# Attention with a feed-forward layer: quad 0's stack of x for the next batch is loaded once x's parts are stored, no longer once q's parts are stored as well

## The reference

```
x = x + attn(layernorm(x));   x = x + ffn(layernorm(x))
attn:  x_h = 16 heads of width 16;  q = x_h @ w_att[h] / sqrt(16)
       att = softmax(q @ x_h^T);  o = att @ (x @ wv^T + b);  o @ out_w^T + out_b
ffn:   silu(fp4(x) @ fp4(w_gate)^T) * (fp4(x) @ fp4(w_up)^T)  ->  fp4(h) @ fp4(w_down)^T
```

## Time and profile before

| | us |
|---|---|
| median of 3 runs | 1467.87 (1466.48 to 1468.46) |
| profiled execution | 1475.75 |
| its span, first to last instruction | 1473.8 |

### The profile page before, as it was taken

How to read it: one execution, slowest core, us unless ns; L and a number is a source line. 1 busy time by engine, 2 the same in 40 slices (tenths; PEclk the granted TensorE clock), 3 DMA queues, 4 the chain that set the end, 5 groups by cost and what they waited for, 6 DMA issues and landing times. The chain is left out here.

```text
span 1473.8 us, 32381 instructions
## 1 busy us (share of the span) xinstructions
PE 1425.4 (97%) x8612; PEld 891.5 (60%) x8612; DVE 1264.4 (86%) x2652; ACT 865.5 (59%) x1731; POOL 659.0 (45%) x911
## 2 busy tenths in 40 slices
PE   6789999999999999999999999899999999999999
PEld 4445555555555555555555554577777777777776
DVE  6878888888888888888888887599999999999996
ACT  1667777777777767777777777533333333333332
POOL 2445545545545546546545523243434343433332
PEclk8999999999999999999999999999999999999999
DMA  7846456455455455465465353000000000000000
GB/s 204 234 132 190 123 144 180 122 154 180 122 154 168 132 155 161 123 166 162 125 165 145 117 145 84 0 15 15 18 14 18 14 18 14 18 14 18 14 18 22
DMA packets 99785, 148.09 MB, mean 100 GB/s; under 512 B 21024, under 2 KB 58272, under 8 KB 99744
## 3 DMA queue, kind: packets, MB, share of 16 engines
q1 hardware_dynamic: 82672, 137.22, 32.9%
q10 hardware_dynamic: 17072, 10.37, 3.0%
HBM read 85.02 MB, written 65.27 MB: 102 GB/s over the span
## 5 line engine op out<-in xcount | busy, mean ns | idle before, releaser
L1189 DVE TENSOR_REDUCE neg_max<-ring 128x1 f32<-128x512 f32 x1016 | 636.3, 680 | 96.2 <-PE ring L919 95.8
L1071 ACT ACTIVATE probs<-scores 128x512 f32<-128x512 f32 x1024 | 533.9, 604 | 184.3 <-PE scores L930 158.4
L1704 PE MATMUL gu_bank<-splits,f_x_T 128*128 128x352 f32 x1024 | 313.7, 459 | 0.1
L919 PE MATMUL ring<-x_stack,q_stack 64*128 64x512 f32 x1016 | 230.1, 449 | 24.5 <-DVE neg_max L1189 11.4
L952 PE MATMUL ring<-probs,v_quad 128*32 128x512 f32 x2048 | 247.9, 602 | 0.2
L1704 PEld LDWEIGHTS gu_bank<-splits,f_x_T 128*128 128x128 f32 x1024 | 189.6, 190 | 95.3 <-ACT f_x_T L1678 0.5
L927 PE MATMUL scores<-q_stack,x_stack 64*128 64x512 f32 x1024 | 207.9, 399 | 10.6 <-DMA max_stack<-max_rows 8.2
L919 PEld LDWEIGHTS ring<-x_stack,q_stack 64*128 64x128 f32 x1016 | 97.8, 186 | 177.2 <-DVE neg_max L1189 114.2
L930 PE MATMUL scores<-max_stack,max_ones 64*128 64x512 f32 x1024 | 203.9, 391 | 0.0
L1394 POOL TENSOR_TENSOR f_small<-f_small,eps 128x1 f32<-128x1 f32 x64 | 43.0, 671 | 296.0 <-DVE f_small L1361 296.0
L1663 ACT ACTIVATE h_T<-h_bank 128x256 f32<-128x256 f32 (+1 forms) x128 | 56.0, 487 | 169.9 <-PE h_bank L1718 169.9
(11 more groups left out here) (144 smaller groups left out, 2014.1 us busy)
## 6 DMA issues: line engine op xcount, KB each, us to landing
x_rows<-splits SPq DMA_DIRECT2D x128, 256.0 KB, 3.9
x_stack<-x_rows SPq DMA_DIRECT2D x126, 256.0 KB, 4.0
q_stack<-q_rows SPq DMA_DIRECT2D x248, 128.0 KB, 4.0
q_rows<-splits SPq DMA_DIRECT2D x64, 256.0 KB, 2.2
out_dram<-x_all SPq DMA_DIRECT2D x64, 128.0 KB, 1.7
x_all<-in_L_attn_x_dram ACTq DMA_DIRECT2D x14, 512.0 KB, 6.9
w_raw<-slabs SPq DMA_DIRECT2D x14, 192.0 KB, 4.0
slabs_kept<-w_turned SPq DMA_DIRECT2D x14, 192.0 KB, 6.1
```

What stands on the lines that cost most here:

```text
L919: pe.matmul(max_bank(b, g, ROWS * n + m)[:, :], row_tile(q_stack[q], m)[:, p, s * P:(s + 1) * P], row_tile(x_stack[q], m)[:, p, :], start= ...
L1071: act.activation(probs[j][:, k, :], scores[k][:, :], ACT.Exp).then_inc(p_ready, 1)
L1189: dve.tensor_reduce(neg_max[q % 2][:, at:at + 1], max_bank(b, g, k)[:, :], AX.X, ALU.max, negate=True).then_inc(m_used, 1)
L1704: m = pe.matmul(gu_bank[c][:, :], x_T[u][:, a, :], gate_up_T[:, a, c * CH:(c + 1) * CH], start=(a == 0), stop=(a == HALVES - 1))
```

## The change

For g = 0 only, SP's stream is written out anew. The four x stores come first, as before. Then SP waits until these four have landed (`stored[0]` at the batch's base plus `X_STORES` = 64), and only then waits for q's parts and stores them. After the wait for `s_ready` it loads x_stack[0] at once; then it waits until all six stores have landed, and loads q_stack[0]. For g = 1, 2 and 3 the stream is as it was. No transfer is added or taken away, and no other engine's stream is touched.

```diff
     LOAD_MAXIMA = 2
+    X_STORES = 4 * 16
...
                 for g in range(QUADS):
                     i = QUADS * b + g
                     if not last:
-                        if g % 2 == 0:
-                            store_half(b + 1, g // 2)
-                        sp.wait_ge(s_ready, QUAD * TT * (i + 1))
-                        load_stacks(sp, b + 1, g, x_stack, q_stack, x_rows, q_rows, stored, stack_loaded)
+                        if g == 0:
+                            store(b + 1, 0, x_rows, "x0", (xh, xl, xl, xh))
+                            sp.wait_ge(stored[0], STORES * (b + 1) + X_STORES)
+                            store(b + 1, 0, q_rows, "q0", (qh, ql))
+                            sp.wait_ge(s_ready, QUAD * TT * (i + 1))
+                            load_x_stack(sp, b + 1, 0, x_stack, x_rows, stack_loaded)
+                            sp.wait_ge(stored[0], STORES * (b + 2))
+                            load_q_stack(sp, b + 1, 0, q_stack, q_rows, stack_loaded)
+                        else:
+                            if g == 2:
+                                store_half(b + 1, 1)
+                            sp.wait_ge(s_ready, QUAD * TT * (i + 1))
+                            load_stacks(sp, b + 1, g, x_stack, q_stack, x_rows, q_rows, stored, stack_loaded)
```

## The result

| | before | after |
|---|---|---|
| median, 14 runs each | 1468.07 us (1464.3 to 1470.73) | 1459.9 us (1457.74 to 1465.71) |
| profiled execution, span | 1475.75, 1473.8 | 1459.96, 1458.0 |

The ratio is 0.9946, with a 95% interval of 0.9934 to 0.9957: 8 us faster. The forecast was faster, 1456 us with a range of 1449 to 1467.

What follows compares the result with a forecast made beforehand. PE, 97% busy, bounds it; usual batches lose time as stack loads delay the maxima's store ACT awaits. Terms 8.5 + 1.5 + 3.0 = 13.0 us off the 1467.87 median give 1454.9, stated as 1456, range 1449 to 1467.

Steps and rivals of the forecast that it cites:

- The mechanism: Quad 1: stack 0's loads delay the maxima's store, holding ACT; batches 1 to 12 lose 0.81 us each, 9.7 in all.
- Rival (a): Something other than the backlog holds the maxima's store, so only batch 0 gains: 1465 us; chance 0.15.
- rival (b): More is won: batch 0's stalls go whole, every batch falls to 54.96 us: 18 us, 1450 us; chance 0.12.
- rival (d): x_stack's loads hold q's landing back by just what they gain, nothing moves: 1468 us; chance 0.08.
- The usual batch: Batches 1 to 12: ACT no longer held at the maxima's store, 0.71 us x 12 = 8.5 us won.
- Batch 13: Written-out batch with the usual pattern, PE waiting up to 1.8 us for max_stack: 1.5 us won.
- Batch 0: Stacks land earlier, cutting PE's 4.02 us stall at step (2, 1) by 2.3, plus 0.7 for clock: 3.0 us.
- a bound of 1 us lost: Batch 0's worst case: x's landing straggles to 64 and q_stack goes out later than before.
- The guess that recording packets lengthens these waits: Offered as perhaps why the profiled execution took 7.9 us above the median; an unrecorded run may then have less to give.
- The landing: Batch 6, quad 1: maxima's store, issued at 398.98, finds clear engines from about 401.1, lands by 402.1 to 402.6.
- the forecast's own sign: Wrong if the distance from maxima's store to its loads in quad 1 stays at 4 us or more.
- rival (c): Slower: the maxima's store waits behind more loads issued ahead and a longer backlog, like batch 9: 1480 us; chance 0.07.

Runs made afterwards that it cites:

- The wait alone: Kernel before, q's stores waiting for x's landing, all loads unmoved: ratio 1.0027 in every batch, 1.0025 only in batch 0, 1.0005 only in batches 1 to 14.
- half 1: Changed kernel with the same order also for x1, q1 and quad 2's stacks: ratio to before 0.9943, 54.96 us a batch.
- q_stack held back: Changed kernel, q_stack[0]'s four loads waiting until quad 1's maxima's store has landed: ratio to before 0.9942, 54.96 us a batch.
- the null: Kernel before against itself, unchanged: ratio 0.9991, 55.33 us a batch in its profile.
- batch 0 alone: Kernel before with the new order only in batch 0, the old one in all later batches: ratio 1.0004.
- later batches alone: Kernel before with the new order only in batches 1 to 14, the old one in batch 0: ratio 0.9958, 54.99 us a batch.

## Why the prediction was right, and which terms were mis-sized

**The mechanism** was right in its main line: the loads of quad 0's stacks held up the maxima's store, ACT waited for it, and the change takes them out of its way. The wait alone, half 1 and q_stack held back each fit this and not the rivals. So do the batches of the old order. In the seven profiles of it named below, the 25 batches with a distance of 4.6 us or more took 56.36 us in the mean, and the 28 with one under 4.1 took 55.02. Rival (a) is out, as the later batches hold the gain and batch 0 none; rival (b) had the usual batch right and batch 0 wrong; rival (d) is out, as q's landing did not move.

One step of it was wrong: how the store is helped. I had it find clear engines sooner. In the 24 batches 1 to 12 of two profiles of the old order (the first and the null), the store's first packet passes 1.75 to 2.5 us after its issue, read in slices of 0.25 us, and the last by 2.75 to 4.5 us. In 24 of the new order (both profiles of the changed kernel) the first passes after 2.0 to 3.0 us, so no sooner, and the last by 3.0 to 3.75. What is won is at the end: the packets no longer pass among q_stack's loads that were issued after the store.

**The usual batch, 8.5 us.** Per batch I forecast 55.06 us; it was 55.01. The gain was over-sized because the earlier trace rows is one execution, and a slow one. Seven profiles with the old order of loads in batches 1 to 12 (the two of before, the null, the three with the wait alone, batch 0 alone) give 55.77, 55.68, 55.33, 55.75, 55.49, 55.31 and 55.52 us a batch, mean 55.55. Four with the new one (the two of after, later batches alone, half 1 too) give 55.01, 55.04, 54.99 and 54.96, mean 55.00. That is 0.55 x 12 = 6.6 us. The new order has also taken most of the scatter away: in the two profiles of the changed kernel these batches run from 54.62 to 55.45 us, where the first profile of before has 54.96 to 56.97.

**Batch 13, 1.5 us.** From its q stores to batch 14's it took 58.26 us in the profile shown, but 54.65 to 56.46 in the six others of the old order; their mean with it is 55.65, the new order's 54.66. So 1.0 us. The seven don't scatter evenly, though. The three profiles of the kernel before itself have 58.26, 56.46 and 56.24 us there, with distances of 5.04 to 5.16; the four edited kernels all have 54.65, with 3.5 to 3.9, though the stack loads follow q's stores as before. By the kernel before alone the term is 2.3 us. Why the edited kernels differ there is open.

**Batch 0, 3.0 us.** This term failed: it is 0 (1.0004). The prediction took a stall of 4.02 us, one event of one execution, as the rule. PE's arrival, 72.00 us in that execution, was 73.1 to 77.2 us in all the others. The prediction also had q_stack go out at 65.0 to 66.0 in batch 0 in spite of the wait for x's landing; in the profiles of the changed kernel it went out at 64.66 and 67.61, in those of batch 0 alone and of half 1 too at 66.98 and 67.74, where the five profiles without the wait have 63.97 to 66.22. It counted the wait only as a bound of 1 us lost; measured, it costs 3.7 us where x_stack isn't moved, and with x_stack moved nothing is lost or won.

**The sum.** 6.6 + 1.0 + 0 = 7.6 us against 8.2 between the medians; with the three profiles of the kernel before alone it is 7.1 + 2.3 + 0 = 9.4. The forecast had 13.0; what it had too much is batch 0's 3.0 and 1.9 of the usual batches. Of the 15.8 us between the two profiled executions, the rest is the first one's bad luck. The guess that recording packets lengthens these waits was wrong.

**The landing.** I had the store land by 402.6 in batch 6's time, 3.6 us after issue, and the distance at 3.4 to 3.7 us in all batches. It was 3.88 there and over 4 in batches 1, 2 and 10 (4.39, 4.00 and 4.06), which by the forecast's own sign would have spoken against it; only batch 1 is clearly longer for it (55.45 us). So ACT is still held by a few tenths, and PE hardly notices. The Trainium skill, "DMA: Bandwidth & Descriptors", section "Queues, rings and completion order", says that an engine takes turns between queues packet by packet. The trace agrees with this only in part. Once the store's packets had begun in the kernel before, they did pass side by side with q1's: 132 beside 129 in the window of the earlier trace rows. But before they begin there is no turn for them: after the change 207 packets of q1 pass in 2.4 us and none of q10, whose store had been issued 0.1 us after the window's start. With q_stack held back, the store's packets began 1.0 to 1.5 us after its issue. Here the measurement decides. The store behaved as if it waited for the loads issued ahead of it, which was half of rival (c); what holds it there, no run shows. The other half of (c), that this backlog would last longer, did not come: against the store's issue its traffic starts about 1.7 us sooner and ends about 1.5 us sooner.

What stays open: why the store's packets take between 0.75 and 2.5 us to pass in batches with the same instructions in the old order, with which the lengths of 55 to 57 us go for the most part; how the wait in batch 0 comes to cost 3.7 us; and whether a semaphore for q's stores is worth anything.

## What to carry to other kernels

In this kernel a small transfer that an in-order engine waits for paid for the bulk traffic issued around it, before and after. Look in the trace for DMA engines that idle shortly before such a collision, and move part of the bulk into that gap; pushing all of it behind the small transfer instead only moved the collision (0.83% slower). Take several profiles before trusting a stall that occurs once: two of three terms here were sized on an unlucky execution. And ask of a stall not only why the data was late but why the engine was early.

## What the runs showed of the hardware

A 16 KB store in pieces of 128 B landed in 2 us with quiet engines. With 256 KB and 128 KB loads issued around it on another queue, ACT came past its wait 3.5 to 5.3 us after the issue, where it comes there itself after about 3.55. The store's first packet passed 1.75 to 3.0 us after the issue with such loads ahead of it, and 1.0 to 1.5 us after it where they were nearly through by then, which I had not expected; with loads issued after it, its packets passed among theirs and took up to 2.5 us.
